# Column sums of B by VectorE and one product, W blocks issued earlier, one unread product added, setup orders placed anew

## What is computed

```python
x = x + _L0_ffn_ref(_L0_cond_ref(x, cond_128, ...), L0_ffn_A, L0_ffn_B, L0_ffn_bias)
x = x + _L1_ffn_ref(_L1_cond_ref(x, cond_128, L1_cond_weight, ...), L1_ffn_W_up, gate_w, ...)

# L0_cond: out = einsum('boi,bih->boh', agg_w, x) + agg_b[:, :, None]
#          agg_w, agg_b: 8 weight sets mixed by a softmax of a small MLP of cond_128
# L0_ffn:  out = x @ (A @ B.T).T + bias          A, B: [1024, 128]
# L1_cond: out = conv1d(x, weight, 9 taps, 4 groups) + (cond_128 @ c_weight.T)[:, :, None] + bias
# L1_ffn:  out = x @ W_up.T + lora_B[e](lora_A[e] x)   e = argmax(x @ gate_w.T + expert_bias)
```

## Time and profile before

| | us |
|---|---|
| median of 3 runs | 1091.26 |
| lowest, highest | 1090.62, 1093.06 |
| the profiled execution | 1094.66 |
| its span | 1092.9 |
| PE busy in the span | 1076.9 |
| DVE busy | 888.6 |
| ACT busy | 588.3 |
| mean granted clock of PE | 0.997 |

### The profile page before, as it was taken

One profiled execution on the slowest core, in us unless ns is written; L12 is line 12 of the kernel. 1 busy time (PEld: TensorE's weight loads), 2 busy tenths in 40 slices (PEclk: granted clock), 3 DMA queues, 4 the chain that ended last, 5 costly groups with the idle time before them and its releaser, 6 DMA issues.

```text
span 1092.9 us, 19053 instructions
## 1 busy us (share of the span) xinstructions
PE 1076.9 (99%) x6987; PEld 1035.6 (95%) x6987; DVE 888.6 (81%) x1644; ACT 588.3 (54%) x1204; POOL 3.6 (0%) x20
## 2 busy tenths in 40 slices
PE   7999999999999999999999999999999999999998
PEld 5788999999999999999999999999999999999998
DVE  3698888888888888888888888888888888888774
ACT  4465555565555565555555555555555555555441
POOL 1000000000000000000000000000000000000000
PEclk8999999999999999999999999999999999999999
DMA  7876544555544555544455544455544555544322
GB/s 275 239 234 165 138 129 118 125 149 159 137 138 112 123 149 157 141 138 113 121 148 156 136 146 111 119 148 157 144 138 113 117 148 155 144 140 95 86 59 78
DMA packets 122844, 152.96 MB, mean 140 GB/s; under 512 B 26272, under 2 KB 95904, under 8 KB 122496
## 3 DMA queue, kind: packets, MB, share of 16 engines
q1 hardware_dynamic: 120416, 147.96, 49.4%
q10 hardware_dynamic: 2336, 3.79, 1.1%
HBM read 81.47 MB, written 36.21 MB: 108 GB/s over the span
## 4 chain that ended last, share of the span: by engine, by line
PE 91%; DVE 4%; DMA 2%; SPq 1%; issue 1%; ACT 0%; DVEq 0%; ACTq 0%
PE M L1580 43%; PE F L1526 8%; PE H L1580 8%; PE F L1468 7%; PE G L1580 7%; PE F L1419 2%; PE F L1417 2%; PE F L1418 2%; PE M L1615 2%; PE G L1500 2%; PE M L1500 2%; DMA x<-in_xP_dram 1%; DMA Lr<-in_Ld_dram 1%; PE F L1451 1%; SPq L317 1%
## 5 line engine op out<-in xcount | busy, mean ns | idle before, releaser
L1580 PE MATMUL M<-Wsh,yh 128*128 128x408 f32 x896 | 320.7, 358 | 0.7 <-DVE x L1093 0.4
L1580 PE MATMUL M<-Wsh,yl 128*128 128x408 f32 x896 | 311.9, 348 | 0.0
L1580 PE MATMUL M<-Wsl,yh 128*128 128x408 f32 x896 | 311.8, 348 | 0.0
L1580 PEld LDWEIGHTS M<-Wsh,yh 128*128 128x128 f32 x896 | 168.8, 188 | 4.5 <-DVE x L1153 0.8
L1027 DVE STREAM_TRANSPOSE yr<-F 128x512 f32<-128x512 f32 x123 | 88.2, 717 | 103.6 <-PE F L1526 103.5
L1580 PEld LDWEIGHTS M<-Wsl,yh 128*128 128x128 f32 x896 | 168.8, 188 | 2.7
L1580 PEld LDWEIGHTS M<-Wsh,yl 128*128 128x128 f32 x896 | 168.5, 188 | 0.3
L525 ACT ACTIVATE yh<-yr 128x1024 fp32r<-128x1024 f32 (+1 forms) x127 | 120.1, 947 | 18.9 <-DVE yr L1042 14.4
L640 ACT ACTIVATE F<-G,cbs 128x128 f32<-128x128 f32 x240 | 67.0, 342 | 70.0 <-PE G L1500 70.0
L525 ACT ACTIVATE F<-biasb 128x512 f32<-128x512 f32 x124 | 74.6, 601 | 46.0 <-DVE yr L1027 45.1
L640 ACT ACTIVATE F<-M,cbs 128x128 f32<-128x128 f32 x240 | 67.0, 342 | 59.2 <-PE M L1500 59.2
(11 more groups left out here) (223 smaller groups left out, 2462.8 us busy)
## 6 DMA issues: line engine op xcount, KB each, us to landing
x<-in_xP_dram SPq DMA_DIRECT2D x64, 516.0 KB, 4.2
xTr<-in_xT_dram SPq DMA_DIRECT2D x64, 512.0 KB, 3.8
Xr<-x SPq DMA_DIRECT2D x502, 64.5 KB, 2.5
out_dram<-x SPq DMA_DIRECT2D x62, 516.0 KB, 3.2
agb<-agb_scratch SPq DMA_DIRECT2D x29, 128.0 KB, 3.4
Wsr<-in_Wsd_dram SPq DMA_DIRECT2D x3, 816.0 KB, 7.7
agg_scratch<-stage ACTq DMA_DIRECT2D x2, 1024.0 KB, 7.2
agg<-agg_scratch SPq DMA_DIRECT2D x58, 32.0 KB, 3.2
```

The lines of the kernel that those rows point to most:

```text
L1580: last = pe.matmul(dst, w[:, y, k, :], m, start=fresh and n_ == 0, stop=k == 3 and n_ == 2, skip_group_check=True)
```

## The change

New tiles: `dum` (128x512, written with ones by POOL ahead of `ident`) and `bsumr` (128x128). What is done otherwise:

- **Column sums.** DVE reduces Br over its eight blocks into bsumr (`bred`), and `bsum` is one product of bsumr with the ones. It waits for v_bs in place of d_b.
- **Unread products.** `fill_pre`, one product of dum with itself in fp32r, stands on PE between the MLP and the transpose of the mixing weights. The old `fill` keeps its size and now stands behind `o_first(0)`. (`fill_post` is defined and not called.)
- **Transfers.** SP loads B behind xT(0, 0) and xT(0, 1), x(0) behind xT(1, 0) and T. It issues gg(2), and x(1) and xT(1, 1) only behind agg_move(1, 0), which waits for v(0). ACT issues w11 and wcl(0) ahead of the first product's copies (`ut(0)` and `tuu(0)` enclose them). w12, wcl(1), w22, x(3), w21 stand ahead of the row copies of sequence 1.
- **Orders.** The setup lists of ACT, DVE, PE and SP are permuted up to the loop; the loop is as it was.

```diff
+            def bred():
+                dve.wait_ge(d_b, 16)
+                dve.tensor_reduce(bsumr[:, :], Br[:, :, :].rearrange("p c r -> p r c"), AX.X, ALU.add).then_inc(v_bs, 1)
...
             def bsum():
 
                 pe.wait_ge(g_con, 4)
-                pe.wait_ge(d_b, 16)
+                pe.wait_ge(v_bs, 1)
                 pe.wait_ge(v_ag, 4)
-                for c in range(8):
-                    last = pe.matmul(M[2][:, 0:2], Br[:, c, :], ones[:, :], start=c == 0, stop=c == 7)
-                last.then_inc(p_cs, 1)
+                pe.matmul(M[2][:, 0:2], bsumr[:, :], ones[:, :], start=True, stop=True).then_inc(p_cs, 1)
...
+            def fill_pre():
+
+                pe.wait_ge(g_dum, 1)
+                pe.matmul(F[0][:, :], dum[:, 0:128], dum[:, :], start=True, stop=True)
...
@@ block.gpsimd
             pool.memset(warmd[:, 1:2], 0.0).then_inc(g_warm, 1)
+            pool.memset(dum[:, :].bitcast(fp32), 1.0).then_inc(g_dum, 1)
@@ block.sync, the setup list
-            sp.dma_start(Br[:, :, :], Bd).then_inc(d_b, 16)
             load_xT(0, 0)
             load_xT(0, 1)
+            sp.dma_start(Br[:, :, :], Bd).then_inc(d_b, 16)
@@ block.scalar, the setup list
-            bh(0)
             evac(2)
             evac(0)
+            bh(0)
@@ block.tensor, the setup list
             pe.matmul(M[1][:, 384:392], h2, W2s, start=False, stop=True).then_inc(p_mlp, 1)
+            fill_pre()
...
             unit_v(0)
-            fill(1, True)
             o_first(0)
+            fill()
             o_first(1)
```

More of the change, by code:

```diff
@@ L144, in adaln_ffn @@
         agb12 = over("agb12", "x1", [128, 512], 4 * 8 * 129)
+        dum = over("dum", "yl", [128, 512], 1728, f32r)
+        bsumr = over("bsumr", "yl", [128, 128], 3344)
         Xr2 = over("Xr2", "yl", [128, 8, 129], 1728)
@@ L1348, in _ @@
             fH(0)
+            xd(2, 0)
             f21(0)
@@ L1649, in agb12, with fill, fill_post @@
                 last.then_inc(p_agb, 1)
-            def fill(n, final=False):
+            def fill():
                 pe.wait_ge(a_b, 1)
                 pe.wait_ge(v_cs, 1)
-                for _ in range(n):
-                    last = pe.matmul(M[2][:, :], Bh[:, 0, :], Bh[:, 0:4, :].rearrange("p c r -> p (c r)"), start=True, stop=True)
-                if final:
-                    last.then_inc(p_fill, 1)
-            def fill_ident(n):
-                pe.wait_ge(g_con, 2)
-                for _ in range(n):
-                    pe.matmul(F[0][:, 0:128], ident[:, :], ident[:, :], start=True, stop=True)
+                pe.matmul(M[2][:, :], Bh[:, 0, :], Bh[:, 0:4, :].rearrange("p c r -> p (c r)"), start=True, stop=True).then_inc(p_fill, 1)
+            def fill_pre():
+                pe.wait_ge(g_dum, 1)
+                pe.matmul(F[0][:, :], dum[:, 0:128], dum[:, :], start=True, stop=True)
+            def fill_post():
+                pe.wait_ge(a_ag, 1)
+                pe.matmul(F[2][:, :], dum[:, 0:128], dum[:, :], start=True, stop=True)
             def cond():
@@ L1708, in _ @@
             c_first(0, 0)
+            c_first(0, 1)
             unit_tu(1)
-            c_first(0, 1)
             unit_v(1)
             c_first(0, 2)
+            row(0, 0, 0)
             unit_o(1, 0)
+            row(0, 0, 1)
             unit_o(1, 1)
-            row(0, 0, 0)
-            row(0, 0, 1)
             row(0, 0, 2)
             row(0, 0, 3)
+            c_first(0, 3)
             unit_o(1, 2)
-            c_first(0, 3)
             for k in range(8):
@@ L1725, in _ @@
             row(0, 1, 1)
+            row(0, 1, 2)
             unit_tu(2)
-            row(0, 1, 2)
             row(0, 1, 3)
-            c_first(1, 0)
             row(0, 2, 0)
@@ L1734, in _ @@
             row(0, 6, 0)
+            c_first(1, 0)
             row(0, 6, 1)
             row(0, 6, 2)
-            unit_v(2)
             row(0, 6, 3)
@@ L1741, in _ @@
             row(0, 8, 2)
-            c_first(1, 1)
+            unit_v(2)
             row(0, 8, 3)
@@ L1747, in _ @@
             row(0, 4, 3)
+            c_first(1, 1)
             row(0, 3, 0)
```

198 lines of the change are left out of this document (101 added, 97 removed).

## The result

| | before | after |
|---|---|---|
| median, us | 1091.49 (4 runs) | 1101.20 (4 runs) |
| lowest to highest | 1090.62 to 1093.06 | 1098.06 to 1101.62 |
| ratio, 95% interval | | 1.0073 (1.0057 to 1.0089) |
| profiled execution, its span | 1094.66, 1092.9 | 1101.03, 1099.3 |
| PE busy in the span | 1076.9 | 1076.9 |

A forecast was written before the change was run, and what follows sets the result against it. TensorE bounds the loop, so only the setup counts: 4.25 less 0.4, about 3.8, plus 1.6 gives 5.4 us; less 1.0 from profile to median, 4.4, so 1086.9 us from 1091.26. Range 1083.3 to 1090.6.

The forecast's parts named there:

- What bounds the kernel: Loop over sequences: bound by TensorE and unchanged, so any shift in entering it reaches the end in full.
- The start's sum, 4.25 us: TensorE, column sums to u_first(1): savings 1.55, 0.46, 1.3 and 1.15, less 0.22 for the fill, start u_first(1) 4.25 us earlier.
- B is loaded behind xT(0,0), xT(0,1): SP's first loads: costs nothing, as the three transfers end at the same byte count and the first product waited for evacuations.
- The clock's 3.0 us: TensorE's first-sequence products: about 3.0 us of the start's gain comes from the clock no longer falling to 0.50.
- rival B: First-sequence products: clock still falls, or timed runs already lack the cold stretch; 3.0 us missing, 1088.6 us, chance 0.25.
- xT(1, 1), 0.4 us: SP, for the middle of u_first(1): issued behind v(0) at 24.0, landing taken as 4.2 us, costs 0.4 us.
- the dense piece: VectorE's nearly full work from 38 to 94 us: starts 3.8 us earlier and loses 1.6 us of idle time.
- VectorE's idle time, 1.6 us: VectorE's dense piece: waits for c_first(0, 3) and x(3) go through earlier SP issues, gaining 1.6 of 2.55 us idle.
- bred, 1.23 us: VectorE's reduction of B before the column sums: 1.23 us, hidden up to 4.3 us, so it costs nothing.
- fill_pre, dum, fill's place: Start: fill_pre fits TensorE's idle time, dum's memset about 0.5 us on POOL, both at nothing; fill's new place costs 0.22.
- Rival C: SP's queue: xT(1, 1) behind the wait for v(0) lands after 11.3 us; slower, 1094.5 us, chance 0.07.
- D: VectorE's dense piece starts earlier but waits more, through ACT's DMA issues and SP's wait in load_B2; 1090.8 us, chance 0.13.

The follow-up runs named there:

- experiment 1: The changed kernel with agg_move(2, 3) put back right behind agg_move(2, 2) on SP; median 1092.19 us, ratio 0.9994 to the kernel before.
- 2, xT(1, 1): The changed kernel with the load of xT(1, 1) back ahead of gg(2) on SP; median 1097.58 us, ratio 1.0036 to the kernel before.
- experiment 4: The changed kernel with agg_move(2, 3) behind agg_move(2, 2), xT(1, 1) ahead of gg(2), B ahead of xT(0, 0); median 1090.76 us, ratio 0.9981.
- experiment 5: The kernel before with only agg_move(2, 3) moved late on SP, behind the LoRA load and rx0(1, 1, 1); median 1099.91 us, ratio 1.0068.
- experiment 7: The kernel before with only the column sums changed: bred on VectorE ahead of alo, one product in bsum; median 1092.67 us, ratio 0.9991.
- experiment 8: Experiment 4 with a fourth move, agg_move(1, 3) right behind agg_move(1, 2) on SP; median 1090.18 us, ratio 0.9979.
- 9, xd: Experiment 8 with VectorE's xd(2, 0) back behind f12(0), as in the kernel before; median 1089.79 us, ratio 0.9975.
- experiment 10: Experiment 8 with the column sums undone: eight products on TensorE, no bred; median 1090.36 us, ratio 0.9991.
- experiment 11: Experiment 8 without fill_pre and the memset of dum, and with fill ahead of o_first(0); median 1090.20 us, ratio 0.9975.
- experiment 12: The kernel of 9, xd with w12 moved behind rx0(0, 1, 1) on SP; median 1090.70 us, ratio 0.9985.
- experiment 6: The changed kernel with ScalarE's agg_out, two DMAs of 1 MB, moved behind vhi(2); median 1096.12 us, ratio 1.0031.

## Why the prediction was wrong

The figures that go with the result are the times of two of VectorE's transposes in each profile: the second y<-F of the first sequence, with which its dense stretch starts, and the last yr<-F ahead of the loop.

| kernel | dense start | last yr<-F | between | median, us |
|---|---|---|---|---|
| before | 37.92 | 85.60 | 47.68 | 1091.49 |
| after | 38.40 | 92.08 | 53.68 | 1101.20 |
| 1, agg_move(2, 3) | 36.07 | 83.36 | 47.29 | 1092.19 |
| 2, xT(1, 1) | 34.46 | 89.02 | 54.56 | 1097.58 |
| 4, three moves | 33.19 | 81.72 | 48.53 | 1090.76 |
| 5, before, late line | 34.43 | 89.89 | 55.46 | 1099.91 |
| 7, before, column sums | 33.77 | 83.06 | 49.29 | 1092.67 |
| 8, four moves | 33.05 | 82.11 | 49.06 | 1090.18 |
| 9, xd | 33.45 | 80.80 | 47.35 | 1089.79 |
| 10, eight products | 34.09 | 80.93 | 46.84 | 1090.36 |

**What bounds the kernel**: right. The loop passed every shift on (959.82 of 960.00 us busy against 959.61), and what happened ahead of it decided.

**The start's sum, 4.25 us**: right between these two profiles, 4.24. Its parts too: 1.56 for the column sums (experiment 10 against 8) and the clock at 1.00. But all of it began 1.07 late: the product of v0 ran at 23.38 (22 to 22.5 forecast) and u_first(1) at 27.14 and not at 26, since "B is loaded behind xT(0,0), xT(0,1)", priced at nothing, cost up to 1.0 us through wk, a transfer that I had not looked at: I compared the byte counts of the three transfers that changed places, not those of their neighbours in front.

**The clock's 3.0 us**: its size was right for one execution and wrong as a gain. From the column sums to u_first(1) the front of before takes 11.57 us with the fall and 8.66 without (experiment 5), 2.9 apart. But both occur with the same code. Each timed run lists its mean granted clock: of 90 runs of before, 42 had 0.999 or more and a mean of 1091.3 us, 34 had 0.998 and 1093.9, 14 less and 1095.3. In the six kernels with the new front and the v(2) wait mended (1, 4, 8, 9, 11, 12), 33 of 71 runs were below 0.999 as well, against 48 of 90. So the change does not take cold stretches away altogether. What does differ is the long ones: at 0.997 or less, like the profiled execution of before, were 14 of 90 runs before and 1 of these 71 (none of 24 in experiments 7 and 10 either). Nor do they stand in the same place: of the 14 profiles only that of before was below 1.00 between 18 and 27 us, while experiment 8 had 0.79 from 36 to 44 and experiment 12 0.74 from 40 to 44. Where the timed runs of before were cold, and why the long stretches are rarer, no run here shows. I took off a third, 1.0, on the way from the profile to the median; most of the rest had to go too. What the prediction called rival B, "the timed runs lack the cold stretch already", was true of 42 runs in 90. The Trainium skill, TensorE: Matmul & The Clock Gate, Part 1, says of a kernel's start that the number of cold products varies from run to run and should not be fitted. The runs show such a spread further in as well, and my forecast had fitted it. The rule on transposes in Part 4 of that page of the Trainium skill did not decide anything: the same two transposes stood in stretches at 0.51 and, in experiment 5, at 1.00.

**xT(1, 1), 0.4 us**: mechanism right, size wrong. It was issued at 25.20 (24.0 forecast) and took

```profile
xTr<-in_xT_dram SPq DMA_DIRECT2D x1, 512.0 KB, 5.9
```

from the view of the DMAs issued from 25 to 26 us; 4.2 was assumed. The two errors of 1.2 and 1.7 us on top of the 0.4, less the 1.1 by which u_first(1) was late itself, made a wait of 2.08 and, behind it, a clock of 0.57 from 32 to 36, which the term had no room for. The choice "nearer the loop's" rested on the traffic before the issue; but x(1) and three agg_moves were issued just ahead of it, from 22.84 on, and five row copies just behind it, from 26.35.

**agg_move(2, 3)**: the step that failed. The sentence "SP now issues xT(2, 0), x(2), Wc(1) and x(3) ahead of the Xr rows [...]; both waits should go" looked at what was moved up and not at what these moves and the permuted tail pushed down. agg_move(2, 3) went from its place right behind agg_move(2, 2) to one behind five row copies, some of which wait for VectorE, and the LoRA load, and so behind agg_out's 2 MB. The prediction weighed gg, xT(1, 1) and load_B2 on that queue and did not name this line, whose consumer, v(2), stands on TensorE and feeds VectorE's dense stretch. The rows were there: issue at 51.80, landing at 58.42, use at 59.59, a slack of 1.2 us for a move of 4.4. It cost 8.6 us (experiment 1), as much as the whole loss against the kernel before (0.0073, 8.0 us), and 7.4 in the reverse. The prediction's sum had no term for it; in its terms the dense piece, forecast 1.6 us shorter than 47.68, was 6.0 longer, 53.68.

**VectorE's idle time, 1.6 us**: the forecast wait for x(3) did go in after, and so did that for c_first(0, 3). In the mended kernels the dense stretch is 47.3 (experiments 1 and 9) and at best 46.84 (experiment 10) against 47.68, so 0.3 to 0.8 were recovered, not 1.6. In those that start early it is longer: 4.15 us earlier at the start became 2.54 at the end in experiment 7, 4.73 became 3.88 in experiment 4. In these profiles the waits for transfers moved and did not vanish.

**bred, 1.23 us**: 1.88, off the path as forecast.

```profile
15.61 1.88 DVE L1238 TENSOR_REDUCE bsumr<-Br 128x128 f32<-128x1024 f32 x1
```

PE reads bsumr at 19.81. That is 1.5 times Al's time. The direction is that of the page of the Trainium skill that the prediction named, but the two rows differ in the operation as well as in the stride, so it is not shown that the stride is the reason. **fill_pre, dum, fill's place**: at nothing, and experiment 11 shows no effect beyond the noise.

**The rivals.** Rival C had the right queue and the right kind (a transfer behind a wait on SP, slower than before, chance 0.07), and for xT(1, 1) it came half true. D named SP's list too, and looked at load_B2. Neither had agg_move(2, 3). And with that line put back the kernel stands at 1092.19, by its ratio 0.6 us faster than before, still above the range; a gain of 4.4 us, as forecast, was not reached by any order of this study (2.7 at best). Most of the clock's 3.0 us was not there to be won in the median.

## What to carry to other kernels

When a queue's list is permuted, make for every DMA a row of three times from the trace (issued, landed, first used) and compare each slack with how far the line moves, for the small DMAs above all; here 16 KB with 1.2 us of slack cost 8 us. Mend a late small transfer by its place in the list, or by moving the large ones issued beside it: in these traces 16 KB took 9.1 us beside 2 MB and 4.2 without. A cold stretch of the clock in one profiled execution is no term of a sum until other runs of the same kernel show it too: the spread of the mean granted clock over the timed runs tells that without a trace.

## What the runs showed of the hardware

- The same wait did and did not cost the clock: 2.08 us idle in u_first(1) was followed by 0.57 from 32 to 36 us in after, while 2.11 us at the same place in experiment 1 left it at 1.00. The same front ran at 0.50 and at 1.00.
- Runs with a mean granted clock of 0.998 were about 2.6 us slower than those with 0.999 or more in the kernel before (34 runs at 1093.9, 42 at 1091.3), and 1.4 slower in the mended ones (32 runs at 1091.3, 38 at 1089.9).
- One 16 KB DMA from a single partition of stage took 4.2 us with nothing large issued beside it on ScalarE's queue (experiment 6), 6.9 and 7.0 in experiments 1 and 5, and 9.1 behind 384 KB and beside 2 MB (after).
- xT(0, 0) and xT(0, 1) ahead of B, all of them issued behind wk, went with a landing of wk's second half at 7.0 to 8.5 us (four profiles) instead of 6.3 to 6.75 (ten profiles). What is issued behind a transfer can delay it.
